# Between two attentions: memory no longer cleared by GpSimd, transposes without a reader, and gates in halves

## The reference

```
x = x + attention0(ln(x))     # 16 heads of 8, rms norm and rope on q and k, causal softmax, projection
x = x + spectral(ln(x)) + b   # FFT, a 128x128 product, inverse FFT: one real matrix "mix"
x = x + linear_attention(ln(x))   # 16 heads of 8: elu+1 on q and k, K^T V, division, projection
x = x + expert_attention(ln(x))   # 8 heads of 64, 5 experts each

ss = sigmoid(x @ Ws); sd = sigmoid(x @ Wd)        # (tokens, head, expert)
ms, md = top-3 masks of ss and sd over the 5 experts
q = sum_e (x @ Wq)[h,e] * sd*md;  k, v = sum_e (x @ Wkv)[h,e] * ss*ms
out = softmax(q k^T / 8) v                        # full attention over 2048 keys
y = sum_h sum_e md[h,e] * (out_h @ Wo)[e]
```

## Time and profile before

| | |
|---|---|
| median of three runs | 1698.67 us |
| all three | 1700.9, 1698.67, 1687.71 us |
| profiled execution | 1687.58 us |
| its span | 1685.8 us |
| TensorE busy | 1556.2 us (92%), mean granted clock 0.966 |
| VectorE, ScalarE, GpSimd busy | 1254.2, 939.7, 847.9 us |

### The profile page before, as it was taken

The page is one execution under the profiler, slowest core; times in us unless marked ns, Lnnn a source line. Parts: engine busy times, 40 slices in busy tenths (PEclk is TensorE's granted clock), DMA queues, the critical chain, the costliest instruction groups (busy, mean ns, idle before and its releaser), DMA issues.

```text
span 1685.8 us, 27140 instructions
## 1 busy us (share of the span) xinstructions
PE 1556.2 (92%) x8404; PEld 1012.7 (60%) x8404; DVE 1254.2 (74%) x2518; ACT 939.7 (56%) x1582; POOL 847.9 (50%) x935
## 2 busy tenths in 40 slices
PE   4699999999999976689999999999999999999998
PEld 2455565565565545466666666567576666666555
DVE  3997787687679536777887778787778787777664
ACT  3446756756755631344655655655655656556652
POOL 2530000000001133458869879788689699698452
PEclk9599999999999987989999999999999999999998
DMA  2000000000000000000000000000000000000000
GB/s 64 0 1 1 2 1 2 1 1 1 1 1 1 1 12 13 1 1 13 0 13 1 1 13 2 0 13 1 13 1 1 13 1 1 1 1 1 1 7 19
DMA packets 12230, 9.39 MB, mean 6 GB/s; under 512 B 3840, under 2 KB 11584, under 8 KB 12096
## 3 DMA queue, kind: packets, MB, share of 16 engines
q1 hardware_dynamic: 12096, 7.66, 1.7%
HBM read 6.61 MB, written 1.05 MB: 5 GB/s over the span
## 4 chain that ended last, share of the span: by engine, by line
PE 63%; POOL 18%; DVE 9%; issue 4%; ACT 4%; SPq 1%; DMA 0%; DVEq 0%; ACTq 0%; POOLq 0%
PE ps L887 10%; PE ps L700 9%; PE ps L734 7%; PE ps L719 7%; PE ps L860 5%; PE ps L875 5%; POOL gs L1526 4%; PE ps L667 4%; PE ps L876 4%; POOL gsum L1527 3%; POOL z L572 3%; POOL onm L566 3%; PE ps L898 2%; POOL h_qk L1528 2%; DVE mxp L1201 2%
## 5 line engine op out<-in xcount | busy, mean ns | idle before, releaser
L1080 ACT ACTIVATE pbuf<-ps 128x512 f32<-128x512 f32 x512 | 301.6, 599 | 170.4 <-PE ps L876 166.2
L976 ACT ACTIVATE pbuf<-ps 128x1024 f32<-128x1024 f32 (+3 forms) x320 | 280.1, 897 | 182.5 <-PE ps L722 92.2
L1201 DVE TENSOR_REDUCE mxp<-ps 128x1 f32<-128x512 f32 (+2 forms) x432 | 279.1, 685 | 82.8 <-PE ps L700 51.4
L1407 DVE TENSOR_TENSOR den<-den,pbuf 128x1024 f32<-128x1024 f32 x224 | 312.8, 1396 | 1.9
L887 PE MATMUL ps<-pbuf,h_v 128*64 128x512 f32 x1024 | 248.7, 606 | 0.0
L1066 ACT ACTIVATE relu<-ps 128x512 f32<-128x512 f32 x256 | 152.2, 599 | 161.2 <-PE ps L860 132.1
L1359 DVE TENSOR_TENSOR gt<-ps,gate 128x320 f32<-128x320 f32 x384 | 181.6, 483 | 78.4 <-POOL h_v L1536 36.4
L700 PE MATMUL ps<-kM,qT 128*128 128x512 f32 (+3 forms) x640 | 230.9, 414 | 9.2 <-ACT kM L963 4.9
L875 PE MATMUL ps<-q1T,k1T 128*128 128x512 f32 x512 | 215.3, 421 | 11.4 <-ACT pbuf L1080 9.9
L1380 DVE CUSTOM_DVE_ANT_0 relu<-ps,relu 128x512 f32<-128x512 f32 x256 | 174.2, 684 | 64.5 <-PE ps L860 61.7
L719 PE MATMUL ps<-qT,kM 128*128 128x512 f32 (+3 forms) x640 | 199.5, 381 | 8.5 <-ACT pbuf L976 8.5
(11 more groups left out here) (224 smaller groups left out, 2799.5 us busy)
## 6 DMA issues: line engine op xcount, KB each, us to landing
wraw<-in_Wkv SPq DMA_DIRECT2D x16, 160.0 KB, 2.5
wraw<-in_Wq SPq DMA_DIRECT2D x8, 160.0 KB, 2.3
out<-x SPq DMA_DIRECT2D x4, 256.0 KB, 2.3
wqkv<-in_wqkvT SPq DMA_DIRECT2D x1, 192.0 KB, 3.9
masks<-in_masks SPq DMA_DIRECT2D x1, 128.0 KB, 4.1
dft<-in_dft SPq DMA_DIRECT2D x1, 128.0 KB, 2.3
wout<-in_Wo SPq DMA_DIRECT2D x2, 64.0 KB, 2.6
ident<-in_ident SPq DMA_DIRECT2D x1, 64.0 KB, 5.8
```

The lines of the kernel that those rows point to most:

```text
L976: nc.scalar.activation(pbuf0[:, u % NP0, :, off:CH], ps[:, b:b + 2, off:CH], ACT.Exp, scale=float(D0) ** -0.5).then_inc(s_exp, 1)
L1080: nc.scalar.activation(pbuf1[:, u % NP1, i, :], ps[:, i, :], ACT.Exp, scale=float(D1) ** -0.5).then_inc(s_exp1, 1)
L1201: v.tensor_reduce(mxp[:, i, h:h + n, b], sc.rearrange("p (h k) -> p h k", h=n), AX.X, ALU.max).then_inc(s_read0d, 1)
L1407: v.tensor_tensor(dn, dn, w, ALU.add).then_inc(s_den1, 1)
```

## The change

Five edits:

1. GpSimd no longer clears between the stages. `sq2` and `rank` are cleared at the step F of the last chunk in SEQ0, as soon as the last scores are there. `z` isn't cleared: in head 0 `by_expert` writes its product straight into z, and there is no addition. The ones of `k2T` are written by ScalarE, in row 64 alone, at the last `pj` step.
2. TensorE gets transposes of `ident` that nobody reads (`keep_clock`), into a free bank: 28 behind the last projection, 20 behind the last mixing, 14 behind the last `lin`, 16 behind the first four projections of head 0, and 18 behind the last F of the program.
3. The logits and gate exponents stand as early as their data allow: those of chunk 0 ahead of the third transposes, and so on.
4. The gates of head 0 are made first and in two halves of 8 tiles, each with its own addition, comparisons, ranks and product. Addition and comparisons of heads 1 to 7 become a step `beats` at place 0.9 of SEQ1, behind the first scores; the ranks go from -0.05 and 2.65 to 2.1 and 3.4.
5. The waits on `s_z` are set for one head's additions fewer, and the first two heads' scores wait for the row of ones.

```
+KEEP = {"pj": 28, "mix": 20, "lin": 14, "gates": 16, "end": 18}
...
-    out += [(-0.05, ("ranks", 1, 4)), (2.65, ("ranks", 4, H1))]
+    out += [(0.9, ("beats",)), (2.1, ("ranks", 1, 4)), (3.4, ("ranks", 4, H1))]
...
         def by_expert(queue, eng, mc, i):
-                eng.tensor_tensor(onm[:, i], on[:, i, :]...
+                eng.tensor_tensor(onm[:, i] if h else z[:, n], on[:, i, :]...
-            if i:
+            if i and h:
...
+            def keep_clock(bank, kind):
+                for _ in range(KEEP[kind]):
+                    pe.transpose(ps[:, bank, 0:P], ident[:], ident[:])
...
+            logits(0)
             transposes3(2)
-            logits(0)
+            logits(1)
+            logits(2)
             transposes3(3)
-            for c in range(1, NC):
-                logits(c)
+            logits(3)
...
+                elif step == ("pj", NC - 1):
+                    for i in range(2):
+                        ins = nc.scalar.activation(k2T[i][D1:D1 + 1, :], ones[D1:D1 + 1, :].to_broadcast([1, T]), ACT.Copy)
+                    ins.then_inc(s_row1, 1)
...
+            gate_exponents(0)
             tokens(2)
+            gate_exponents(1)
+            gate_exponents(2)
             tokens(3)
+            gate_exponents(3)
...
-            dve.wait_ge(s_g2, NC)
-            link(v.tensor_scalar(gate[:], gate[:], 1.0, None, ALU.add))
+            for half in range(2):
+                tiles = slice(NT // 2 * half, NT // 2 * (half + 1))
+                dve.wait_ge(s_g2, NC // 2 * (half + 1))
+                link(beaten(slice(0, 1), tiles))
+                link(ranks(v, link, slice(0, 1), tiles))
+                gates(0, tiles)
...
+                elif step == ("F", NG - 1, NC - 1):
+                    pool.wait_ge(s_sc, 2 * N0 * NG)
+                    g_.memset(sq2[:], 0.0)
+                    for e in range(E1):
+                        ins = g_.memset(rank[:, :, :, e:e + 1], float(e))
...
-            g_.memset(z[:], 0.0)
-            g_.memset(sq2[:], 0.0)
-            for e in range(E1):
-                g_.memset(rank[:, :, :, e:e + 1], float(e))
-            for i in range(2):
-                ins = g_.memset(k2T[i][:].bitcast(F32), 1.0)
```

75 lines of the change are left out of this document (45 added, 30 removed).

## The result

The changed kernel takes 1686.69 us (median of 7 runs, 1679.67 to 1689.82), the kernel before 1698.25 us (7 runs beside them). The ratio is 0.9948, with a 95% interval from 0.9926 to 0.9971: 8.8 us won, between 5 and 13, where I had forecast 18. The profiled execution took 1679.67 us; its span of 1677.8 us is 8.0 us shorter than the one before.

What follows compares the result with a forecast made beforehand. TensorE is 92% busy; bridge and tail are bound by a chain of small waiting steps at low clock. 5.2 + 3.1 + 1.0 + 4.1 + 1.7 + 1.5 = 16.6 us put the median at 1682.1; forecast 1680, range 1664 to 1695.

Steps and rivals of the forecast that it cites:

- rival C: Start of second attention: GpSimd and VectorE take back all earlier-gate gain, z gives nothing; 12.7 us won, 1684; chance 0.2.
- Rival A: Bridge: the clock holds through the 3.3 us gap too; 5 us more, 21.6 in all, 1675 us; chance 0.15.
- Term 3: Head 0's gates in halves: ready 3.7 us earlier, 2 (0 to 4) given back in VectorE's queue; net gain 1.7 us.
- Term 4: Second attention: z written, not added to, in head 0; 16 GpSimd additions leave; gain 1.5 us (0 to 3.4).
- Term 1: Bridge: GpSimd's clearing leaves the chain, so VectorE's step at L1261 takes 0.29 us instead of 5.46; gain 5.2 us.
- the middle of term 2: Bridge, 615 to 631 us: transposes in the gaps keep the clock at full; gain 3.1 us.
- A clock of 0.5 in the middle of a fill: Sign of being wrong in the new profile; expected was clock 1.0 from 611 to about 630 us.
- Rival B: All fills: transposes do not hold the clock; 4.7 us left, 1692 us; chance 0.1.
- The gap of 3 us: Before the last key-value matmuls: 14 transposes too few, TensorE idle 3.3 us, clock falls; gain 1 of 0 to 6.
- The tail: Very end: 18 transposes fill the gap before z's transposes and hold the clock; gain 4.1 us.

Runs made afterwards that it cites:

- e6: Changed kernel without any of its extra transposes (all five fills set to 0); 1688.98 us, ratio 0.9967 to the kernel before.
- changed again: One more execution of the same changed kernel, nothing altered; it took 1687.93 us.
- f1: Changed kernel with GpSimd's clearing of z, sq2, rank and both k2T back in its old place and order; 1690.13 us, ratio 0.9978.
- e1: Changed kernel with the comparisons of heads 1 to 7 ahead of the first score matmul (place -0.05 instead of 0.9); 1684.66 us, ratio 0.9935.
- e2: Changed kernel with the ranks of heads 1 to 3 at 7.3 and 4 to 7 at 9.5, instead of 2.1 and 3.4; 1688.71 us, ratio 0.9958.
- e5: e4 with comparisons of heads 1 to 7 in three pieces before VectorE's idle times, ranks at -0.05 and 2.65; 1669.65 us, ratio 0.9871.
- second pair: One more execution each of the kernel before and the changed kernel, both unaltered; 1694.13 and 1687.93 us.
- e7: e4 with GpSimd's xl subtractions early, without waiting for the last xn; 1672.60 us, ratio 0.9876.
- e8: Changed kernel with only the clearing of both k2T by GpSimd put back; 1686.17 us, ratio 0.9942.
- e4: Changed kernel with 40 instead of 14 transposes in the fill before the last key-value matmuls; 1675.42 us, ratio 0.9894.
- e3: Changed kernel with GpSimd's xl subtractions of chunks 1 to 3 waiting until head 0's gates are through; 1689.32 us, ratio 0.9967.
- g2: Kernel before with only the reordered logits, exponents, halved gates, comparisons and ranks; clearing, z and fills as before; 1701.46 us, ratio 1.0054.
- h1: Changed kernel with comparisons of heads 1 to 7 in three pieces before VectorE's idle times, ranks at -0.05 and 2.65; 1680.57 us, ratio 0.9917.

## Why the prediction was right and wrong

The forecast was 1680 us, 18 less than before; 1686.7 came, 8.8 less by the ratio (11.6 by the medians). In the profiled pair the sum was 16.6, and 8.0 came. Two figures of the prediction don't follow from its own terms: rival C makes 13.1 us and not 12.7 (16.6 less 2.0 and 1.5), and A with the better bounds of terms 3 and 4 reaches 1671 and not 1668. Neither changes the forecast.

**Term 1 and the middle of term 2, right.** 5.2 + 3.1 = 8.3 us was predicted up to the end of kf; stage A gave 8.1 in the profiled pair. The split is 3.7 to 4.7 for the clearing (before against e6, changed again against f1), where 5.2 stood, and the rest for the clock, so part of the agreement of the sum is luck. It is not always all of it: in some executions the clock falls at the last projection or ahead of it and comes back only in the middle of the fill, and A is 27.2 instead of 25.4 us (changed again, e1, e2, e5). The second pair of executions has 6.3 us in stage A. A clock of 0.5 in the middle of a fill was one of my signs of being wrong.

What the stalls show, L1292's 4.11 us that end with GpSimd's memsets, and the steps of 0.2 us that take 1.2 beside xl, is a wait for whole instructions, no slower step. The Trainium skill (SBUF — State Buffer, section "SBUF: two separate sides") has a rule for this: a VectorE instruction in a two-port mode, or one with two SBUF inputs beside a GpSimd instruction that reads SBUF, shares a port pair with GpSimd as an exclusive lock for the whole instruction. The comparisons and ranks beside xl in the changed kernel and in e7 have two SBUF inputs and agree with it. So does f1, where a sum of two SBUF tensors (`qfT<-lt`) took 0.67 us beside memsets, which read nothing, and the same sum takes 0.68 alone. L1292 (L1261 before) has one tensor and a constant as input; which mode it ran in, the trace does not show. That the wait goes on through a whole row of memsets is what f1 and the second execution of the kernel before show. The steps that read PSUM beside e8's memset took 0.41 to 0.75 us, as elsewhere.

**Rival B, wrong.** Transposes hold the clock: 1.00 through 3.22 us of them in the changed kernel, and through 4.53 in e4. They also let it come back: in the second execution of the changed kernel the clock was 0.50 up to 619.7 us, of which the last 3.1 us were transposes of the fill alone, and 1.00 from there on, within the same fill. In e4's tail nothing but the fill of 18 ran from 1662.1 to 1665.5 us at 0.50, and then the clock was at 1.00. Without fills (e6) it was low there for 13.7 us and then for 6.8 more, and A is 29.9 us. The sentence of the Trainium skill (TensorE: Matmul & The Clock Gate, Part 4: PE-mode transpose) that speaks against it isn't borne out for these 128x128 transposes in fp32.

**The gap of 3 us, right.** The fill of 14 was too few, the clock fell behind it, and of the predicted 1.0 us 0.8 came (0.4 in the second pair). Rival A asked what a clock that holds would give: 5 us more. It was more: 11.3 by e4's median, 9.2 by its ratio. I had counted from the profiled execution, with B at 30.7, and not seen that B is 34 to 37 us in most executions without a hold.

**Term 3, the step that failed.** The mechanism was named, and both its sizes were off.

- The 3.7 us of earlier gates. "4.5 us for a half" was right for the instructions (e3: 4.5, the second half 4.0), and GpSimd's xl was not looked at. It had stood there before as well, beside nothing that mattered, in the 5.14 us for which VectorE was idle ahead of the gates. With the gates moved forward they met it. 3.7 us were predicted and 1.0 came; with xl moved, C gives 4.5.
- "I take 2 of the 3.7 us back (0 to 4)": it was 7.0, in all eight executions with this order beside the other parts, and 8.5 in g2. The comparisons take 4.6 us with their addition (713.31 to 717.9), and the ranks of heads 1 to 3, 4.2 us from 721.29 on, had lain ahead of the first gt of the stretch, where VectorE now stands idle for 2.94 us. That makes 8.8 us moved into the queue of the gt, and 7.0 of them arrived at the end of the eight units. I had taken a part of the 3.6 us alone, as if VectorE had room because it is busy for 33 of 43 us. A busy share of 76% is no room where the busy time sets when banks come free.

Net, the term was +1.7 in the prediction and is -6.0 in stages C and E of the pair, -6.7 with D; alone, on the kernel before, it makes the kernel 9 us slower (g2). h1 has this order mended, and its median is 1680.57 us where the forecast had 1680. By its ratio it is 14.1 us under the kernel before, not 18, so the mended order gives somewhat over half of what was missing, and the nearness of the two medians is in part luck.

**Rival C** (this part and z give nothing) was the nearest, with 1684, and too mild by the same 3 us; z gave its part.

**Term 4, right in kind, too low:** 1.5 (0 to 3.4) was predicted and 2.1 came up to unit 32. Another 1.1 us came behind it, and no run shows from what.

**The tail, right in the profiled pair:** 4.1 predicted, 3.9 measured in T, and 4.2 against e6. In the second execution of the kernel before T is 24.6 us, and the second pair gives 1.5: there, too, the low clock is a draw, and part of the gain is only had in some executions. In e2, e4 and e7 the clock fell just as the fill of 18 began, behind matmuls without a pause. The fill then stood on the chain of waits for 3.6 to 3.7 us, where it takes 2.2 beside it at the full clock, and T is 24.5 us, about as long as without fills in that execution of the kernel before.

The sum over the stages of the pair is 8.1 + 0.8 + 1.0 - 0.6 - 7.0 + 2.1 + 1.1 + 3.9 = 9.4 us; the changed execution was 1.4 us later at the start of stage A, which leaves 8.0.

## What to carry to other kernels

Where work is moved from a place in which its engine's partner waits into one in which that engine frees buffers, price it in full, whatever its busy share says; the idle times in the timeline row by row are the places to put it, in pieces that fit. A step moved forward meets other neighbours: look at what GpSimd does at the new time before counting VectorE's instructions. And where the clock can fall behind an idle time, the length of the low stretch in one profiled execution is one draw: fill the gap up to its end, and look for the gain in the median more than in the pair of traces. Whether the small gaps behind it are worth filling too is open here.

## What the runs showed of the hardware that was not expected

- Back-to-back transposes of 128x128 in fp32 held the granted clock at 1.00 for 4.53 us (40 of them, in all eight kernels with this fill), and it rose from 0.50 to 1.00 in the middle of a row of 28, 3.1 us of which had gone by (changed again).
- With the same instructions ahead, the clock behind kf stayed at 1.00 or fell: of the eight kernels with the fill of 40, six held it (B 24.4 to 27.2 us) and two did not (34.4 and 35.2). What differed at that moment isn't seen in the rows; the two with small fills as well both held it.
- The clock also fell without an idle time just ahead of it: at 1662.1 us in e4, where TensorE had been busy for all of the 7.1 us before, at 1.00.
- Single VectorE steps of 0.2 us took 1.2 beside a GpSimd subtraction of 1.27 us, and steps of 0.29 us took 4.11 to 5.88 beside rows of memsets; the step waits until the row is through, so a short step can pay twenty times its length.
